# Gated attention on one Trainium2 core: scores through one matrix per head, in float32r high and low parts

## The reference, cut to what matters

```python
gate_v = _get_sel_gate(x, sel_v_w, rs)     # top 2 of 8 sigmoids per head, normalized
gate_o = _get_sel_gate(x, sel_o_w, rs)
q = jnp.einsum('bsd,hpd->bhsp', x, q_w.reshape(H, P, D))
k = jnp.einsum('bsd,hpd->bhsp', x, k_w.reshape(H, P, D))
xv = jnp.einsum('bsd,hedp->bshep', x, v_w.reshape(H, E, D, P))
v = jnp.einsum('bshep,bshe->bhsp', xv, gate_v)
att = jax.nn.softmax(jnp.einsum('bhqp,bhkp->bhqk', q, k) * SCALE, axis=-1)
ctx = jnp.einsum('bhqk,bhkp->bqhp', att, v)
weighted = ctx[:, :, :, None, :] * gate_o[..., None]
out = jnp.einsum('bshep,hepd->bsd', weighted, o_w.reshape(H, E, P, D))
```

## Time and profile before

| what | value |
|---|---|
| three runs, us | 1202.22, 1204.62, 1211.36 (median 1204.62) |
| the profiled execution's span, us | 1202.7 |
| the stage of the change in it | about 512 to 841 us |

### The profile page before, as it was taken

One profiled execution on the slowest core, in us unless ns is written; L12 is line 12 of the kernel. 1 busy time (PEld: TensorE's weight loads), 2 busy tenths in 40 slices (PEclk: granted clock), 3 DMA queues, 4 the chain that ended last, 5 costly groups with the idle time before them and its releaser, 6 DMA issues.

```text
span 1202.7 us, 18102 instructions
## 1 busy us (share of the span) xinstructions
PE 1047.4 (87%) x5942; PEld 735.0 (61%) x5942; DVE 811.3 (67%) x1977; ACT 665.8 (55%) x1640; POOL 387.2 (32%) x608
## 2 busy tenths in 40 slices
PE   3587899999976989878899999998699899999677
PEld 2345677777741333655667677776568566668565
DVE  5763588887866867258788777667755566665563
ACT  3253566666642757456677877777134466665121
POOL 5220112111111101034655657557300344443200
PEclk8687799999985989989899999999599999999779
DMA  6503000000004330030000000030600100000000
GB/s 217 111 10 104 1 1 6 9 1 1 1 26 145 132 91 3 1 140 1 1 1 1 1 1 1 1 140 1 251 1 2 72 2 1 2 1 2 1 1 18
DMA packets 26572, 45.08 MB, mean 37 GB/s; under 512 B 3536, under 2 KB 23792, under 8 KB 25200
## 3 DMA queue, kind: packets, MB, share of 16 engines
q1 hardware_dynamic: 23936, 41.57, 10.2%
q10 hardware_dynamic: 2544, 2.36, 0.6%
HBM read 36.94 MB, written 6.82 MB: 36 GB/s over the span
## 4 chain that ended last, share of the span: by engine, by line
PE 41%; ACT 9%; DVE 8%; issue 3%; POOL 2%; DMA 1%; DVEq 0%; SPq 0%; ACTq 0%; POOLq 0%
PE psum L1736 7%; ACT region_d L1802 4%; PE psum L2397 3%; PE psum L2450 3%; PE psum L2381 2%; ACT region_c L1819 2%; PE psum L2364 2%; PE psum L1773 2%; PE psum L1750 2%; PE psum L2359 2%; PE psum L2807 1%; PE psum L409 1%; PE psum L2356 1%; PE psum L2404 1%; PE psum L1053 1%
## 5 line engine op out<-in xcount | busy, mean ns | idle before, releaser
L1736 PE MATMUL psum<-gated_parts 128*128 128x512 f32 x768 | 198.8, 412 | 15.0 <-DVE region_d L1906 10.9
L1736 PEld LDWEIGHTS psum<-gated_parts 128*128 128x128 f32 x768 | 141.3, 192 | 68.3 <-DVE region_d L1906 30.9
L1987 POOL TENSOR_TENSOR region_d<-region_d 128x256 f32<-128x256 f32 x126 | 99.5, 790 | 114.4 <-DVE region_d L1906 114.0
L1434 ACT ACTIVATE rounds_work<-psum,region_c 128x512 f32<-128x512 f32 x128 | 87.0, 689 | 59.3 <-PE psum L1349 59.3
L787 DVE TENSOR_REDUCE work<-psum 128x1 f32<-128x512 f32 x128 | 81.8, 685 | 28.0 <-PE psum L365 26.4
L1359 PE MATMUL psum<-parts,split 128*128 128x512 f32 x384 | 97.6, 404 | 0.0
L1802 ACT ACTIVATE region_d<-psum,gated_work 128x128 f32<-128x128 f32 x256 | 75.8, 451 | 36.8 <-issue 26.2
L1349 PE MATMUL psum<-parts,split 128*128 128x512 f32 x384 | 94.4, 396 | 0.0
L1590 POOL CAST parts<-rounds_work 128x1024 fp32r<-128x1024 f32 x32 | 33.4, 1044 | 179.7 <-ACT rounds_work L1434 179.7
L1504 DVE TENSOR_TENSOR parts<-rounds_work,parts 128x1024 fp32r<-128x1024 f32 x64 | 77.5, 1223 | 20.3 <-POOL parts L1590 17.4
L1906 DVE SCALAR_TENSOR_TENSOR region_d<-psum,gated_work,region_d 128x128 f32<-128x128 f32 x256 | 71.4, 344 | 29.0 <-ACT region_d L1802 20.6
(11 more groups left out here) (433 smaller groups left out, 2189.4 us busy)
## 6 DMA issues: line engine op xcount, KB each, us to landing
region_a<-in_l1v SPq DMA_DIRECT2D x1, 4096.0 KB, 14.4
region_b_last<-in_l1o SPq DMA_DIRECT2D x1, 4096.0 KB, 12.4
region_a<-in_l2f SPq DMA_DIRECT2D x1, 4096.0 KB, 13.5
region_b_last<-in_l3f_small SPq DMA_DIRECT2D x1, 4096.0 KB, 19.8
region_a<-in_l3f SPq DMA_DIRECT2D x1, 2080.0 KB, 7.3
region_c<-in_l0f SPq DMA_DIRECT2D x1, 2076.0 KB, 12.2
region_c<-in_l3x SPq DMA_DIRECT2D x1, 2048.0 KB, 7.9
ctx_parts<-front_work SPq DMA_DIRECT2D x6, 256.0 KB, 3.8
```

The lines of the kernel that those rows point to most:

```text
L1434: act.activation(H[g % 2][:, f, :], bank[f], ACT.Gelu_apprx_tanh, bias=W("b1")[:, (g % E) * FT + f:(g % E) * FT + f + 1]).then_inc(h_ready ...
L1736: ins = pe.matmul(bank[2 * (n % 2) + c], src[a][:, t * P:(t + 1) * P], weights[b][:, piece(c)], start=m == 0, stop=m == len(PASSES) - 1)
L1987: pool.tensor_tensor(tile[:, 0:2, :], tile[:, 0:2, :], tile[:, 2:4, :], ALU.add).then_inc(k.pool_chain, 1)
```

## The change

For every head the query and key weights are multiplied on TensorE at the start of the stage (eight float32 matmuls of 128 columns into banks 0 and 1). ScalarE takes out the high part with the scale folded in, VectorE the low part (`m_part`). The weights are laid out differently on the host for this; their load has the same size.

In every turn `query_rows(h)` makes the scored side from `m_part` and `x_part` in float32r, three passes for each of two pieces of 512 tokens. ScalarE makes its high part, VectorE its low part (`low_rows(h)`, `u_part`). `scores(h, b)` multiplies `u_part` with `x_part` in three float32r passes of 256 columns. No keys are made, and `qT` and `kT` are gone. On VectorE `low_rows(h)` is the first thing of a turn, ahead of `select` and of the first `merge`; `select(0)` is moved behind `low_rows(0)`.

```diff
     def tensor(pe):
         bank = k.bank
+        pe.wait_ge(k.weights[name], 16)
+        pe.wait_ge(k.x_tiles, NT * number)
+        for h in range(NH):
+            ins = pe.matmul(bank[h // 4][:, (h % 4) * P:(h % 4 + 1) * P], W("q")[:, h, :], W("k")[:, h, :],
+                            start=True, stop=True)
+            if h % 4 == 3:
+                ins.then_inc(m_psum.semaphore, 1)
         k.norm.tensor(pe, use, k.xn)
-        pe.wait_ge(k.weights[name], 16)
...
-        def queries_and_keys(h):
-            for i in range(4):
-                if h == 0 and i == 2:
-                    pe.wait_ge(probs_ready, 1)
+        def query_rows(h):
+            if h == 0:
+                pe.wait_ge(*m_high.at(2))
+                pe.wait_ge(*m_low.at(2))
+                pe.wait_ge(*x_low.at(2))
+            for c in range(2):
                 if h > 0:
-                    pe.wait_ge(*o_low.at(B * (h - 1) + i + 1))
-                pe.matmul(bank[4 + i], W("q" if i < 2 else "k")[:, h, :], k.xnT[:, (i % 2) * HALF:(i % 2 + 1) * HALF],
-                          start=True, stop=True).then_inc(qk_psum, 1)
+                    pe.wait_ge(*o_low.at(B * (h - 1) + c + 1))
+                for n, (a, b) in enumerate(PASSES):
+                    ins = pe.matmul(bank[4 + c], m_part[a][:, h * P:(h + 1) * P], x_part[b][:, piece(c)],
+                                    start=n == 0, stop=n == len(PASSES) - 1)
+                ins.then_inc(u_psum, 1)
+
+        def scores(h, b):
+            if b < 2:
+                pe.wait_ge(*u_low.at(2 * h + b + 1))
+            elif h > 0:
+                pe.wait_ge(*o_low.at(B * (h - 1) + b + 1))
+            elif b == 2:
+                pe.wait_ge(probs_ready, 1)
+            for t in range(TPB):
+                tt = b * TPB + t
+                for n, (a, c) in enumerate(PASSES):
+                    ins = pe.matmul(bank[4 + b][:, t * S:(t + 1) * S], u_part[a][:, tt * P:(tt + 1) * P],
+                                    x_part[c][:, b * S:(b + 1) * S], start=n == 0, stop=n == len(PASSES) - 1)
+            ins.then_inc(score_psum, 1)
...
@@ scalar
+        for c in range(2):
+            act.wait_ge(*m_psum.at(c + 1))
+            act.activation(m_part[0][:, piece(c)], bank[c], ACT.Copy, scale=scale).then_inc(m_high.semaphore, 1)
...
-                for i in range(4):
-                    act.wait_ge(qk_psum, 4 * h + i + 1)
-                    dst = (qT if i < 2 else kT)[h % 2]
-                    act.activation(dst[:, (i % 2) * HALF:(i % 2 + 1) * HALF], bank[4 + i], ACT.Copy,
-                                   scale=scale if i < 2 else 1.0).then_inc(qk_sb, 1)
+                for c in range(2):
+                    act.wait_ge(u_psum, 2 * h + c + 1)
+                    if h > 0 and c == 0:
+                        act.wait_ge(score_psum, B * h)
+                    act.activation(u_part[0][:, piece(c)], bank[4 + c], ACT.Copy).then_inc(u_high, 1)
@@ vector
         k.norm.vector(dve, chain, use, k.x, k.xn, 1e-5)
+        for c in range(2):
+            dve.wait_ge(*m_high.at(c + 1))
+            dve.scalar_tensor_tensor(out=m_part[1][:, piece(c)], in0=bank[c], scalar=scale, in1=m_part[0][:, piece(c)].bitcast(F32),
+                                     op0=ALU.mult, op1=ALU.subtract).then_inc(m_low.semaphore, 1)
...
+        def low_rows(h):
+
+            for c in range(2):
+                dve.wait_ge(u_high, 2 * h + c + 1)
+                if h > 0 and c == 0:
+                    dve.wait_ge(score_psum, B * h)
+                dve.tensor_tensor(u_part[1][:, piece(c)], bank[4 + c], u_part[0][:, piece(c)].bitcast(F32), ALU.subtract)\
+                    .then_inc(u_low.semaphore, 1)
...
-        select(0)
...
         for h in range(NH + 1):
+            if h < NH:
+                low_rows(h)
             if h == 0:
+                dve.wait_ge(probs_ready, 1)
+                select(0)
                 maxima(h)
...
-GATED_PARTS = 10 * 1024
+GATED_PARTS = 14 * 1024
```

More of the change, by code:

```diff
@@ L1641, in gated_attention @@
     k.carve_from(0)
-    qT, kT, V = ([k.carve(F32, T) for _ in range(2)] for _ in range(3))
+    at = 6 * T + 4 * WIDE
+    u_part = [parts[:, at + i * T:at + (i + 1) * T] for i in range(2)]
+    m_part = [parts[:, at + (2 + i) * T:at + (3 + i) * T] for i in range(2)]
+    V = [k.carve(F32, T) for _ in range(2)]
     PR, PT = (k.region["C"][:, i * B * TPB * S:(i + 1) * B * TPB * S].rearrange("p (b t n) -> p b t n", b=B, t=TPB)
@@ L1667, in gated_attention @@
     probs_ready = sem("probs_ready")
-    qk_psum = sem("qk_psum")
-    qk_sb = sem("qk_sb")
+    m_psum = k.count("rounds_chooser", 2)
+    m_high = k.count("rounds_zeros", 2)
+    m_low = k.count("rounds_rows_psum", 2)
+    u_psum = sem("u_psum")
+    u_high = sem("u_high")
+    u_low = k.count("rounds_h_low", 2 * NH)
     ex_psum = sem("ex_psum")
@@ L1741, in tensor @@
             if h < NH:
-                queries_and_keys(h)
+                query_rows(h)
                 if h > 0:
@@ L1745, in tensor @@
                 for b in range(B):
[L1746 to L1752, removed]
+                    scores(h, b)
                 if h == 0:
-                    pe.wait_ge(*x_low.at(2))
                     experts(values_block(h), x_part)
@@ L1860, in vector @@
         k.norm.vector(dve, chain, use, k.x, k.xn, 1e-5)
+        for c in range(2):
+            dve.wait_ge(*m_high.at(c + 1))
+            dve.scalar_tensor_tensor(out=m_part[1][:, piece(c)], in0=bank[c], scalar=scale, in1=m_part[0][:, piece(c)].bitcast(F32),
+                                     op0=ALU.mult, op1=ALU.subtract).then_inc(m_low.semaphore, 1)
         dve.wait_ge(k.weights[name], 16)
-        dve.wait_ge(probs_ready, 1)
+        def low_rows(h):
[5 more added lines that the diff above has]
+                    .then_inc(u_low.semaphore, 1)
         def select(n):
@@ L3366, in pack @@
                  columns(f["L0_ffn_b1"]), columns(f["L0_ffn_b2"]), across(np.arange(4, 0, -1, dtype=np.float32))]
-    by_head = lambda a: a.reshape(8, P, D).transpose(2, 0, 1).reshape(P, -1)
+    by_head = lambda a: a.reshape(8, P, D).transpose(1, 0, 2).reshape(P, -1)
     w["l1f"] = [by_head(f["L1_ffn_q_w"]), by_head(f["L1_ffn_k_w"]), f["L1_ffn_sel_v_w"].T, f["L1_ffn_sel_o_w"].T,
```

## The result

| | median us | runs | profiled span us |
|---|---|---|---|
| before | 1205.8 | 11 | 1202.7 |
| after | 1213.48 | 11 | 1210.3 |

The ratio is 1.0072, with a 95% interval of 1.0049 to 1.0094: 0.7% slower. That is inside the range of the prediction and less than 1%, and the interval leaves out no change. One of the 11 executions after the change, 1227.54 us, fell in the chip's slower state and is left out of the ratio.

What follows compares the result with a forecast made beforehand. TensorE, busy 87% of 1202.7 us, was taken as the bound, with VectorE's first merge deciding when the value block ends in heads 2 to 5. Terms summed to +11.6, span 1214.3; adding 1.9 gave 1216 us, range 1204 to 1224.

Steps and rivals of the forecast that it cites:

- head 0: Start of the stage: ScalarE has its gates 1.2 us earlier and paces this block; 1.0 us gained.
- head 1: `select` starts later, +2.0; its 2.13 us stall and the slow stretch behind it grow, +0.3; scores gain nothing: +2.3 us.
- heads 2 to 5: Each: +2.0 for the later `select`, +2.4 for slow matmuls, -0.55 for scores, so +3.85 us; +15.4 together.
- heads 6 and 7: Without `select`, each saves 2.0 us on projections and 0.55 on scores, -2.55; -5.1 us together.
- the forecast cost of 0 for the eight matmuls: Start of the stage: the per-head matrices are made while TensorE waits for the norm; uncovered, at most 3.75 us.
- The savings on TensorE: Per head: projections from 3.43 to 1.4 us, 2.0 less; scores from 3.45 to 2.9 us, 0.55 less.
- the upper bound of 0.153 from half-array pairs: Scores: price per 256-column float32r matmul from 258-column matmuls paired on half arrays; 3.7 us a head, 0.2 more than before.
- The delay on VectorE: Head 3's value block: low parts start `select` and the first merge 2.0 us later; TensorE's stall grows from 0.65 to 4.65 us.
- The slow clock: Value blocks of heads 2 to 5: matmuls behind the longer stall run at 1.2 GHz, costing 2.4 us each; range 0 to 3.
- The clock that holds: Rival: same delays in heads 2 to 5, but TensorE keeps 2.4 GHz, four times 2.4 less: 1206.5 us; chance 0.22.
- Dear short matmuls: Rival: score matmuls cost 0.153 us each, six heads lose 0.8 more each: 1221 us, chance 0.13; extreme 1231 us, chance 0.03.
- the vector engine that doesn't decide: Rival: low parts fit VectorE's idle time between `low_outputs`, first merge no later, heads 1 to 7 keep 2.55: 1186 us; chance 0.09.

Runs made afterwards that it cites:

- The second profile: The changed kernel itself, with nothing altered, profiled once more: 1210.1 us in all.
- late low parts: Changed kernel with the query rows' low parts in heads 1 to 5 moved behind the value block's third and seventh merges: 1199.6 us, ratio 0.993.
- delayed `select`: Kernel before, with three chained additions over 512 columns on VectorE ahead of `select` in heads 1 to 5: 1223.4 us, ratio 1.0117.

## Why the prediction was right, point by point

| term | forecast | profile |
|---|---|---|
| head 0 | -1.0 | -1.2 |
| head 1 | +2.3 | +1.8 |
| heads 2 to 5 | +15.4 | +12.5 |
| heads 6 and 7 | -5.1 | -5.2 |
| together | +11.6 | +7.9 |

Head 0 is taken from the start of the gate product to the first values product; the others are differences of the turns. The mechanism came as forecast, every sign too. The sum came 3.7 us too high.

The spans differ by 7.6 us, which looks like the 7.9 but is so by luck. The gate product starts 1.7 us later in the profile after, because the stages ahead, which are the same code, ended 1.9 us later; from their last matmuls to the gate product the changed kernel lost nothing, so the forecast cost of 0 for the eight matmuls held. Behind the last values product the profile after is 2.0 us shorter, in code that is again the same. Head 0 holds luck as well: its -1.2 has the slow clock behind the 1.42 us stall in it, and in the two executions without that it took 27.2 and 27.3 us, not 29.0. The median was missed by 2.5 us only, because it lay 3.2 us above the profiled span and not 1.9.

**The savings on TensorE** were as worked out. Query rows 1.39 us (1.4 forecast), scores 2.87 (2.9). The price read down from 384 to 256 columns was 0.12 a matmul; L1753 starts every 0.119, and the upper bound of 0.153 from half-array pairs did not apply. The rule of the Trainium skill ("TensorE: Matmul & The Clock Gate", Part 3, "Packing small matmuls") that a weight load overlaps a running matmul only in another row group does not hold here. Each of these full-height matmuls has its own load, recorded at 0.19 us, and they start every 0.119 us.

**The delay on VectorE** is the step that decided the sign. `select` was to start 2.0 us later and did so by 2.06, counted from TensorE's first matmul of the queries or query rows; the stall was to be 4.65 us and was 4.57. That it is the cause, and not just beside it, rests on three runs: moved away, it gives back 1.4%; put alone into the old kernel, it costs 1.2% (both with the slow clock that comes with it); with `select` out of its way, the change is 18 us faster.

**The slow clock** was the term that was mis-sized. I took 2.4 us a turn, near the stall of 4.93 us in the earlier trace rows, whose 33 matmuls took 10.48 us against 8.09 in head 3. It was 1.5 in two heads and 2.2 in the two others, 1.85 on average. Over four heads that is 2.2 of the 3.7 us by which the sum was high. It is real: filling the stall gives 0.8% back. The second profile, with the dearer kind in all four heads, reaches 2.3, so the term was too high by the luck of the profile in part. One working in the prediction is slightly off: 15 matmuls at 0.245 us are 3.7 us, not 3.6, so the shorter stall cost 1.8 us more than its length, not 1.9. The sum doesn't use it.

**Head 1** was 0.5 us better than forecast. TensorE resumed 2.1 us later in the turn, as forecast, and its first stall grew from 2.13 to 6.24 us. But the slow stretch behind did not grow (36 matmuls in 10.40 us, 10.54 before), so the 0.3 for it did not come. **Heads 2 to 5** resume 1.9 us later when it is counted from the start of the turn and not 2.0, because the query rows begin 0.2 us earlier behind the values product than the queries did. For head 3 the terms then close: 1.88 of delay, less 0.59 for the scores and the boundary behind them, plus 1.50 of clock make 2.79, and the turn grew by 2.79.

**The rivals.** The clock that holds (0.22) is out by the granted clock, and its 1206.5 us is 7 below the median. With the stall filled, its condition was made true, and the kernel took 1206.5 us; that it is the same to the tenth is chance, since the kernel before took 1207.7 on that chip. Dear short matmuls and the vector engine that doesn't decide are out by the rows above. My chances put 0.41 on slower by over 1%, which the measured 0.7% is not; with the clock at 1.85 the sum would have been 1214 and that chance smaller.

## What to carry to other kernels

Before taking work from the busiest engine, look at what the busiest engine is waiting for in each part of the loop. Where another engine's queue releases it, an operation put at the head of that queue costs its full length and its wait, though that engine is idle for a fifth of the turn; its place in the queue is worth more than its size. A chain of small dependent operations is best cut up and laid where its engine waits anyway: here that turned a change that was 0.7% slower into one that is 1.6% faster than the kernel before. Laid between operations that the busiest engine waits for, the same chain costs: head 0 got 5 to 6 us longer by it.

## What the runs showed of the hardware

A stall of TensorE can cost more than its length: the 33 matmuls behind a 4.6 us stall lost another 1.5 to 2.3 us at 1.2 GHz, and matmuls that nobody reads, run inside the stall, gave it back. The cost was 1.5 us where the clock fell within 1 us of TensorE's resuming, and 2.2 to 2.3 where it had fallen 1.6 to 1.9 us before.

The length of a stall did not decide alone whether the clock fell. The half clock followed stalls of 2.13 and 2.48 us and all eight of 2.8 us. It followed none of eleven of 2.7 us. The same 1.42 us stall in the same code had it in four executions of six. The two kernels whose stalls were all alike (late low parts, delayed `select`) repeated one outcome in every head and in both executions, where I had taken it for chance from stall to stall. That the place in time decides is likely and not shown.

float32r matmuls of 256 columns with a weight load each start every 0.119 us, those of 512 every 0.23 to 0.24.
